# Attention and ternary feed-forward on one core: the low parts of K's first block subtracted one place earlier in VectorE's order

## What is computed

```python
q, k, v = proj(x, Wq), proj(x, Wk), proj(x, Wv)          # 16 heads of 64
q = q * jnp.minimum(cond_1, 4.0)
scores = jnp.einsum('bhqd,bhkd->bhqk', q, k) / np.sqrt(64)
attn = softmax(where(causal, scores, min))
a = einsum('bhqk,bhkd->bhqd', attn, v)  ->  einsum('bsd,ed->bse', a, Wo)
q_w = clip(round(weight / alpha), -1, 1) * alpha          # ternary weight
q_x = clip(round(a / scale), -128, 127) * scale           # per row
out = x + einsum('bsi,oi->bso', q_x, q_w) + bias
```

## Time and profile before

| what | value |
|---|---|
| median of 3 runs | 2042.46 us (2041.6 to 2043.03) |
| the profiled execution, its own time | 2044.32 us |
| its span, first to last instruction | 2042.3 us |
| TensorE busy, VectorE busy | 95%, 66% of the span |
| ScalarE busy, GpSimd busy | 50%, 45% |
| the chain that ended last, share on TensorE | 82% |

### The profile page before, as it was taken

One profiled execution on the slowest core, in us unless ns is written; L12 is line 12 of the kernel. 1 busy time (PEld: TensorE's weight loads), 2 busy tenths in 40 slices (PEclk: granted clock), 3 DMA queues, 4 the chain that ended last, 5 costly groups with the idle time before them and its releaser, 6 DMA issues.

```text
span 2042.3 us, 40256 instructions
## 1 busy us (share of the span) xinstructions
PE 1935.3 (95%) x12347; PEld 1697.0 (83%) x12378; DVE 1357.6 (66%) x3330; ACT 1027.5 (50%) x2495; POOL 916.2 (45%) x985
## 2 busy tenths in 40 slices
PE   8999889899998999998999999999988999999998
PEld 6788667899998999998999988999976777777775
DVE  6545665477778777788777787777777545454554
ACT  4443333377677776777777777777774000000000
POOL 1333443344446444465444455444454544444441
PEclk9999989899999999999999999999999999999999
DMA  6899998877777867777778777786772332323332
GB/s 216 327 374 350 343 344 313 300 270 242 271 267 264 284 246 269 275 254 260 274 261 287 233 273 261 256 286 236 277 242 76 118 110 92 123 92 116 100 101 73
DMA packets 165696, 477.83 MB, mean 234 GB/s; under 512 B 12768, under 2 KB 84448, under 8 KB 135776
## 3 DMA queue, kind: packets, MB, share of 16 engines
q1 hardware_dynamic: 165072, 476.11, 66.5%
q10 hardware_dynamic: 528, 0.52, 0.1%
HBM read 331.88 MB, written 111.15 MB: 217 GB/s over the span
## 4 chain that ended last, share of the span: by engine, by line
PE 82%; DVE 7%; DMA 4%; issue 3%; ACT 2%; POOL 2%; SPq 0%; DVEq 0%; ACTq 0%; POOLq 0%
PE proj_ps L211 26%; PE s_ps L598 9%; PE proj_ps L598 8%; PE o_ps L377 7%; PE t_ps L339 6%; PE t_ps L1012 6%; PE o_ps L669 5%; PE o_ps L1012 4%; PE s_ps L299 3%; PE s_ps L300 3%; DMA xv_raw<-xT 2%; DVE pt_all L363 2%; DMA parts<-x_scratch 2%; DVE prob L311 1%; DVE xv L910 1%
## 5 line engine op out<-in xcount | busy, mean ns | idle before, releaser
L211 PE MATMUL proj_ps<-parts 128*128 128x256 f32 x5376 | 770.2, 291 | 15.2 <-DMA parts<-x_scratch 10.0
L211 PEld LDWEIGHTS proj_ps<-parts 128*128 128x128 f32 x5376 | 678.5, 192 | 27.3 <-issue 10.5
L329 POOL TENSOR_TENSOR prob<-prob,row_inv 128x128 f32<-128x128 f32 (+3 forms) x512 | 376.9, 736 | 597.6 <-DVE row_inv L323 597.2
L317 ACT ACTIVATE prob<-prob,row_min 128x128 f32<-128x128 f32 (+3 forms) x512 | 287.6, 562 | 175.1 <-DVE row_min L311 167.8
L363 DVE TENSOR_TENSOR pt_all<-t_ps,pt_all 128x128 fp32r<-128x128 f32 (+3 forms) x512 | 249.4, 487 | 108.0 <-ACT pt_all L356 106.8
L339 PE MATMUL t_ps<-ident,prob 128*128 128x128 f32 x1280 | 229.3, 277 | 49.4 <-DVE pt_all L363 42.0
L311 DVE CUSTOM_DVE_ANT_0 prob<-s_ps,mask 128x128 f32<-128x128 f32 (+3 forms) x512 | 247.8, 484 | 34.1 <-PE s_ps L300 6.9
L654 ACT ACTIVATE yt_q<-t_ps 128x1024 bf16<-128x1024 bf16 x32 | 32.8, 1024 | 426.6 <-PE t_ps L647 426.6
L356 ACT ACTIVATE pt_all<-t_ps 128x128 fp32r<-128x128 f32 (+3 forms) x512 | 217.1, 424 | 8.5 <-PE t_ps L339 6.1
L339 PEld LDWEIGHTS t_ps<-ident,prob 128*128 128x128 f32 x1280 | 153.2, 142 | 72.4 <-issue 47.7
L598 PE MATMUL proj_ps<-wo_parts,o_parts 128*128 128x512 f32 x768 | 187.5, 398 | 0.0
(11 more groups left out here) (126 smaller groups left out, 2824.2 us busy)
## 6 DMA issues: line engine op xcount, KB each, us to landing
parts<-x_scratch SPq DMA_DIRECT2D x224, 1024.0 KB, 7.9
x_scratch<-xv SPq DMA_DIRECT2D x112, 512.0 KB, 5.9
k_sw<-k_st SPq DMA_DIRECT2D x128, 256.0 KB, 3.7
xv_raw<-xT SPq DMA_DIRECT2D x17, 1024.0 KB, 8.8
v_scratch<-v_tmp SPq DMA_DIRECT2D x64, 256.0 KB, 5.3
v_raw<-v_scratch SPq DMA_DIRECT2D x32, 512.0 KB, 3.9
oT_scratch<-o_sum SPq DMA_DIRECT2D x64, 256.0 KB, 2.6
o_raw<-oT_scratch SPq DMA_DIRECT2D x32, 512.0 KB, 4.6
```

Source lines behind the costliest of these rows:

```text
L211: mm = pe.matmul(qk_bank(w, m), wc[w][:, c, wp, k, :], xq[:, c, :, xp, k, :], start=(fresh and k == 0 and i == 0), stop=(k == CH - 1 and i ...
L317: act.activation(prob[u % QT], prob[u % QT], ACT.Exp, bias=row_min[:, u % 4:u % 4 + 1], scale=-1.0, accum_out=row_sum[:, u % 4:u % 4 + 1]) ...
L329: pool.tensor_tensor(prob[u % QT], prob[u % QT], row_inv[:, u % 4:u % 4 + 1].broadcast_to([P, w]), ALU.mult).then_inc(norm_done, 1)
```

## The change

VectorE subtracts the low parts of K's first block (two L280 instructions) in front of L(6), not behind M(10). All other work keeps its order, on VectorE and on the other engines. No instruction is added or taken away.

```diff
@@ dve_step
             I(8)
             M(9)
             W(11)
+            evacuate(now, K, 0)
             L(6)
             I(9)
             M(10)
-            evacuate(now, K, 0)
             if last and now:
                 o_low_part(dve, 0, 0)
             W(12)
             L(7)
```

## The result

| | before | after |
|---|---|---|
| median of four runs each | 2042.74 us (2041.6 to 2046.93) | 2012.8 us (2010.29 to 2015.62) |
| ratio of the two, 95% interval | | 0.985 [0.9831, 0.987] |
| the profiled execution, its span | 2044.32, 2042.3 us | 2013.7, 2011.6 us |

What follows compares the result with a forecast made beforehand. TensorE, busy 95%, was taken as the bound, stalling at T(9) for L(7) behind the pair. Gains of 25.8 + 3.6 + 1.1 = 30.5 us from a median of 2042.46 gave 2012.0 us, range 2008 to 2024.

Steps and rivals of the forecast that it cites:

- T(9) in 27 steps, less T(8): Regular steps: T(9)'s stall behind L(7) goes, 27.2 us by starts, less 1.4 for T(8): 25.8 us gained.
- three `late_for` steps at J(24): J(24) waits for W(12), which comes 1.17 us earlier; 1.2 us taken for each step, 3.6 together.
- last step: Stall of 2.21 us at T(9): L(7) comes 1.40 earlier, less L(6)'s delay of 0.3, 1.1 us gained.
- Starts against the idle column: Regular steps' T(9) stalls priced by quarter starts, 1.03 us a step and 27.2 in all; idle column says 0.87 and 22.9.
- The cover and T(8): Pair runs while VectorE waits for H(6); L(6) is 0.27 us late, T(8) loses 0.05 a step, 1.4 in all.
- The rival at T(8): Pair beside GpSimd's N(8) takes 0.45 us longer, moving the stall to T(8) in part: 2024 us; chance 0.10.
- The rest of the J(24) stall: In the `late_for` steps part of the stall at J(24) stays, about 0.5 to 0.8 us.
- a pair at half speed: Pair in its new place takes 2.8 us, T(8) loses more than T(9) gives back: 2051 us; chance 0.05.

Runs made afterwards that it cites:

- experiment 3: Kernel before, each L280 of the pair in its old place preceded by a throw-away row reduction; 2098.36 us, ratio 1.0266.
- 1: Changed kernel with the pair moved behind L(6), ahead of I(9) and M(10); 2036.28 us, ratio 0.9957 to the kernel before.
- 6: Changed kernel with the pair moved behind L(7), in front of I(10); 2020.39 us, ratio 0.989 to the kernel before.
- Experiment 4: Changed kernel, but the `late_for` steps and the last step keep the old order; 2020.31 us, ratio 0.9882 to the kernel before.
- experiment 8: Changed kernel with the first L276 of Q's second block moved up in front of I(3); 2006.88 us, ratio 0.9828 to the kernel before.

## Why the prediction was right

**The bound.** T(9) waited for the pair in front of L(7), and in regular steps next to nothing took its place. That the pair's length there set the time is shown by experiment 3 (longer pair, quarter 9.67 to 10.93) and the removal by 1, 6 and the change.

**Term by term**, by the S(12) intervals:

| term | forecast | measured |
|---|---|---|
| T(9) in 27 steps, less T(8) | 25.8 | 25.6: 19.29 in 20 intervals, 1.56 in those that end in `qk_for`, 3 x 1.39 in the quarter that fell from 10.53 to 9.14 in the next ones, 0.60 in the last but one |
| three `late_for` steps at J(24) | 3.6 | 3.3: quarters 12.01, 12.37, 12.02 to 11.06, 11.03, 11.04 |
| last step | 1.1 | 0.9 |
| not forecast | | 1.5, a drop of the clock that went |
| sum | 30.5 | 31.3 |

The first term held because two misses cancel. By the quarters T(9) gave 28.2 us where 27.2 were worked out, since it gave 1.39 to 1.41 and not 1.0 in each of the three steps with `qk_for`. T(8) and T(5) in their quarter took 2.6 where 1.4 were taken off: 0.7 in the 20 regular steps, 1.5 in the three with `qk_for`, 0.4 in the last but one. In the last step the quarter with T(9) fell from 10.33 to 8.65, 1.7 where 1.1 were worked out, but its last quarter rose from 8.14 to 9.75. Experiment 4, with the old order in the last step alone, has the last two intervals as before (80.68 against 80.67), so their split into 0.60 and 0.9 means little.

**Starts against the idle column.** By the idle column the regular steps would have given 22.9 us, by the starts 27.2 before T(8)'s part. In the 20 regular steps the quarter gave 0.86 to 1.06, 1.00 in the mean, so the starts were right. The Trainium skill (Perfetto Trace Analysis, Per-instruction lifecycle) calls the end that a profile gives a TensorE instruction an estimate; the trace agrees: 0.87 us of the idle column were 1.03 by the starts.

**The cover and T(8).** L(6) was to be 2.09 us behind ScalarE's pair and was 2.21, since the pair took 1.53 and not 1.41. T(8) was put at 0.05. In the group of the rows shown the quarter rose by 0.11 at most (8.86 to 8.97); in experiment 6, where nothing delays T(8), it is 8.85 to 8.87 there. In the other three groups it rose by 0.00 to 0.03 in the mean. So the mean of all 20 is near 0.04, and in experiment 8, with T(5)'s wait gone, no quarter of a regular step shows any of it.

**The rival at T(8)** came true in three steps. In a `qk_for` step GpSimd is behind: it is still at a part of V (L435) when the pair starts, and N(8) lands in the middle of the pair:

```profile
619.87 1.10 POOL L435 TENSOR_TENSOR v_st<-v_raw,v_st 128x256 fp32r<-128x256 f32 x1
620.52 1.80 DVE L280 TENSOR_TENSOR k_st<-k_sum,k_st 64x512 fp32r<-64x512 f32 x2
...
620.93 0.85 POOL L329 TENSOR_TENSOR prob<-prob,row_inv 128x128 f32<-128x128 f32 x1
...
623.06 0.30 PE L339 MATMUL t_ps<-ident,prob 128*128 128x128 f32 x1 [0.30 <-DVE pt_all L363]
```

The quarter went from 9.37 to 9.84, 0.47 us given back. The rival had the right size for one such step (0.45) but the wrong number of steps, and that is what kept the time at 2012 and not 2024. The size was right by luck: the prediction had N(8) as the only neighbour, and of the 0.4 us by which this pair is longer, 0.3 are in its first instruction, beside L435.

**What the prediction had loosely.** The rest of the J(24) stall was put at 0.5 to 0.8. The idle column shows 0.30 in each of the three, here the first:

```profile
663.45 0.95 PE L211 MATMUL proj_ps<-parts 128*128 128x256 f32 x6 [0.30 <-DVE parts L483]
```

By the quarters the gain was 0.95, 1.34 and 0.98, near the 1.2. And the drop of the clock was not seen, though it stood in the trace of before. Windows of a microsecond there, behind the longest of the J(24) stalls:

```profile
963.00:964.00 1.00, 0.27 (x2) 0.30 (x3) 1.00 (x2) 0.00 (x0) 0.00 (x0) 1.00 0.08 33
964.00:965.00 1.00, 1.00 (x9) 1.00 (x8) 1.00 (x5) 0.12 (x1) 0.67 (x1) 0.75 1.01 205
965.00:966.00 1.00, 1.00 (x7) 1.00 (x6) 1.00 (x3) 0.96 (x3) 0.16 (x1) 0.50 0.97 270
```

That step's next interval is 36.09 before and 34.59 after, and 36.12 in experiment 4, which keeps the stall. Without these 1.5 us, which are luck, the intervals would give 29.8, against 30.5 forecast.

## To carry to other kernels

An instruction on an engine that is not the bound costs time only where it stands directly ahead of something the bound waits for; put it into an idle time of its engine, between its own input and the next thing wanted, where it costs little as long as it fits (here L(6) came 0.39 us later behind a pair of 1.53, and TensorE lost 0.04 of it in a regular step) and one for one what goes beyond. Behind the wanted instruction it looks as good in a regular step, but the fullest kind of step and the DMA queue behind it decide. Price a stall by the starts of like stretches, with and without it, and look at the granted clock behind the longest ones.

## What the runs showed of the hardware

**A low part of VectorE's and a GpSimd operation exclude each other, as far as the rows go.** The prediction thought of a pair that is slowed over its length. The rows say that it is held until GpSimd's operation is over: in the step shown N(8) ends at 765.01 and the pair at 766.28, 1.27 later. A second one, of the changed kernel, group 3:

```profile
1014.76 0.40 POOL L329 TENSOR_TENSOR prob<-prob,row_inv 128x128 f32<-128x128 f32 x1
1015.01 1.42 DVE L280 TENSOR_TENSOR k_st<-k_sum,k_st 64x512 fp32r<-64x512 f32 x2 [0.61 <-ACT k_st L268]
```

N(8) ends at 1015.16, the pair at 1016.43, 1.27 later again. In the earlier trace rows the operation ends at 1533.18 and the pair at 1534.45, once more 1.27. Sixteen pairs of the changed kernel begin more than 0.13 before the end of a GpSimd operation and have no second one beside them; all end 1.26 or 1.27 behind it. With a pair of 1.40 us alone, that is as if it started in earnest 0.13 before GpSimd's recorded end, however long that operation was. The overlap differs between the groups, and the pair with it: where it starts 0.26 before N(8)'s end it is recorded with 1.53, where it starts 0.15 before, with 1.42. In the `qk_for` step shown, the two instructions of the pair by themselves:

```profile
620.52 0.99 DVE L280 TENSOR_TENSOR k_st<-k_sum,k_st 64x512 fp32r<-64x512 f32 x1
621.54 0.78 DVE L280 TENSOR_TENSOR k_st<-k_sum,k_st 64x512 fp32r<-64x512 f32 x1
```

The first ends at 621.51, 0.54 behind L435 (620.97), and the second at 622.32, 0.54 behind N(8) (621.78); 0.69 from 0.13 before each end would give 0.56. N(8) itself is recorded with 0.85, not 0.39, beside the first. The Trainium skill (SBUF — State Buffer, Who interferes with whom) has a VectorE instruction with two SBUF inputs contend with a GpSimd one that reads SBUF, and calls it an exclusive lock; the trace agrees in all these places. So the price of a neighbour on GpSimd is what is left of its operation, and the long pair of the earlier trace rows was no sign of a pair at half speed. No run here varied the overlap on purpose.

**The clock can fall behind short stalls.** Behind idle times of 1.98 us (before) and 2.14 us (experiment 3) the granted clock went to 0.50 for about 3 us and cost up to 1.5 us; behind the 0.87 us stalls it was 1.00. Not every stall of 2 us did it (14 of 23 in experiment 3 did not), and what sets that stayed open.
